# Routing the second part of a mixture-of-experts kernel in two batches in place of one

## What is computed

```python
x = x + conv(ln_c(x))              # per row i: q, k, v, gate g from 64 channels, 4 heads of 32
    # scores = q.k * scale + bias ; a = softmax(scores) ; o = g * (a.v) ; project back to 64 channels
t = x.reshape(64 * 128, 128)       # 8192 tokens
xf = layernorm(t)
gate_logits = xf @ Wg + bg                           # 8 experts
top_w, top_i = top_k(gate_logits, 2); top_w = softmax(top_w)
for e in range(8):
    h = gelu(xf @ W1[e] + b1[e])                     # 128 -> 512
    out += w_dense[:, e:e+1] * (h @ W2[e] + b2[e])   # 512 -> 128
return t + out
```

## Time and profile before

| | |
|---|---|
| median of three executions | 930.24 us (928.44 to 931.15) |
| the profiled execution | 927.51 us, of which 925.7 us from first to last instruction (the span) |
| busy, of the span | DVE 715.3 us (77%), PE 671.7 (73%), ACT 600.8 (65%), POOL 476.7 (52%) |
| granted TensorE clock, mean | 0.887 of full speed |
| chain that ended last | PE 54%, DVE 26%, issue 6%, POOL 6%, DMA 4%, SP's queue 2% |

### The profile page before, as it was taken

The page is one execution under the profiler, slowest core; times in us unless marked ns, Lnnn a source line. Parts: engine busy times, 40 slices in busy tenths (PEclk is TensorE's granted clock), DMA queues, the critical chain, the costliest instruction groups (busy, mean ns, idle before and its releaser), DMA issues.

```text
span 925.7 us, 22535 instructions
## 1 busy us (share of the span) xinstructions
PE 671.7 (73%) x7125; PEld 539.0 (58%) x7125; DVE 715.3 (77%) x2447; ACT 600.8 (65%) x1502; POOL 476.7 (52%) x550
## 2 busy tenths in 40 slices
PE   0006698988799678867897753629999999999900
PEld 0001477777577456646675642518888888888800
DVE  3798488888888797878777858478888888888843
ACT  0015489999699576856785674227888888888700
POOL 4000133444564356736865587005777777777770
PEclk9999699999899898978987875559999999999965
DMA  9932750000000000000000013225422214464178
GB/s 200 221 86 54 189 85 2 2 2 2 1 2 2 1 1 25 25 0 17 28 19 24 16 44 89 50 50 142 111 77 80 65 52 134 111 161 120 50 212 238
DMA packets 66936, 64.53 MB, mean 70 GB/s; under 512 B 21637, under 2 KB 58054, under 8 KB 65288
## 3 DMA queue, kind: packets, MB, share of 16 engines
q1 hardware_dynamic: 56392, 35.95, 16.7%
q0 software_dynamic: 9152, 18.76, 6.2%
q10 hardware_dynamic: 1280, 8.39, 4.0%
HBM read 35.88 MB, written 26.93 MB: 68 GB/s over the span
## 4 chain that ended last, share of the span: by engine, by line
PE 54%; DVE 26%; issue 6%; POOL 6%; DMA 4%; SPq 2%; ACT 1%; POOLq 0%; ACTq 0%; DVEq 0%
PE PT L1459 12%; PE S L1305 4%; PE PT L1315 4%; PE B L1343 4%; PE S L1444 4%; PE S L1446 4%; PE S L1445 4%; DVE L L969 3%; PE PT L1451 2%; DMA xt<-in_x 2%; DVE on L982 2%; PE A L1274 2%; DVE xt L990 2%; DVE pl L956 2%; POOL expert_out L698 2%
## 5 line engine op out<-in xcount | busy, mean ns | idle before, releaser
L857 ACT ACTIVATE hf<-S,b_sb,inv_hscale 128x256 f32<-128x256 f32 x312 | 150.8, 564 | 28.7 <-PE S L1446 28.7
L667 POOL DMA_INDIRECT routed<-pay,pos x128 | 127.5, 996 | 68.9 <-issue 31.5
L969 DVE CUSTOM_DVE_ANT_0 L<-S,biasN,logit_scale 128x128 f32<-128x128 f32 x512 | 148.3, 345 | 16.5 <-issue 14.9
L776 ACT ACTIVATE L<-L,lmin 128x128 f32<-128x128 f32 x512 | 159.2, 391 | 0.4
L651 POOL TENSOR_TENSOR og<-gt,on 128x256 f32<-128x256 f32 x64 | 46.5, 726 | 163.3 <-DVE on L982 163.1
L698 POOL DMA_INDIRECT expert_out<-pay x108 | 112.7, 1043 | 32.9 <-issue 26.5
L1212 DVE SCALAR_TENSOR_TENSOR hl<-hf,hscale,hh 128x512 f16<-128x512 f32 x156 | 117.2, 751 | 5.6
L1210 DVE TENSOR_SCALAR hh<-hf,hscale 128x512 f16<-128x512 f32 x156 | 75.4, 484 | 41.7 <-ACT hf L857 41.7
L771 ACT ACTIVATE ph<-PT 128x512 f16<-128x512 f32 x128 | 75.9, 595 | 27.8 <-PE B L1332 19.6
L1459 PE MATMUL PT<-w_h,hh 128*128 x624 | 86.5, 220 | 2.3 <-DVE hl L1212 2.3
L956 DVE TENSOR_TENSOR pl<-PT,ph 128x512 f16<-128x512 f32 x128 | 83.5, 682 | 4.6 <-ACT ph L771 4.6
(11 more groups left out here) (241 smaller groups left out, 1812.0 us busy)
## 6 DMA issues: line engine op xcount, KB each, us to landing
pay<-routed SPq DMA_DIRECT2D x54, 130.0 KB
shared<-expert_out SPq DMA_DIRECT2D x12, 384.0 KB, 6.6
xt<-in_x SPq DMA_DIRECT2D x8, 512.0 KB, 24.5
shared<-in_L_conv_ln_w ACTq DMA_DIRECT2D x8, 512.0 KB, 12.1
shared<-in_L_conv_ln_b ACTq DMA_DIRECT2D x8, 512.0 KB, 10.4
shared<-in_L_ffn_W SPq DMA_DIRECT2D x8, 512.0 KB, 7.2
routed<-blank SPq DMA_DIRECT2D x30, 129.0 KB, 2.6
shared<-expert_out SPq DMA_DIRECT2D x16, 224.0 KB, 5.5
```

The lines of the kernel that those rows point to most:

```text
L667: pool.indirect_dma_start(routed[TABLE_OF[b]], bass.IndirectOffsetOnAxis(ap=pos[k][:, row:row + 1], axis=0), source[:, part_row(b, i), :], ...
L776: last = nc.scalar.activation(L[p][:, h, i, :], L[p][:, h, i, :], ACT.Exp, scale=-1.0, bias=lmin[p][:, h * R + i:h * R + i + 1])
L857: last = nc.scalar.activation(hf[p][:, b, :], S[2 * p + pair][:, k * TILE:(k + 1) * TILE], ACT.Gelu, scale=inv_hscale[:, 0:1], bias=b1_fla ...
L969: last = nc.vector.tensor_tensor_reduce(out=L[p][:, h, i, :], in0=S[h][:, i * P:(i + 1) * P], in1=biasN[:, h, :], scale=logit_scale[:, 0:1 ...
```

## The change

The 24 rows of the fourth batch become a batch of 8 (rows 40 to 47) and a last one of 16 (rows 48 to 63). Both go to table 1, and the numbers of tiles, 47 and 31, are as they were.

- The batch of 8 is routed inside attention. By `plan` its `scale_rows` stands at the end of step 27, its rows at steps 28 and 29, turning at 29 and 30, gate logits at 30 and 31, the halves of `pick` at 31 and 32, ranks and positions at 33, ahead of `tile_table(0)` in the same step. The ranks of batch 2 stand in step 30 too; gate logits therefore get other columns of the bank (`GATE_AT`), and PE waits for DVE to have taken them before it starts the ranks.
- Its rows have a payload of their own for each choice, in `rows_all`: POOL normalises each row twice, and both choices can be sent without `second_choice`. Of its 16 transfers four stand in step 34, and the other twelve behind attention, after the twelve left of batch 2.
- The transition handles 16 rows in place of 24: four groups in place of six. The transfers among the tiles are 32 in place of 48, spread over the same 29 tiles.
- The slots of the tiles change order: `pay[0]` is used first and `rows_all` from the twentieth tile on, ahead of which SP waits for the 16 transfers. Buffers move (`L0`, the junk of the squares).

```diff
-    BATCHES = ((0, 16), (16, 12), (28, 12), (40, 24))
-    TABLE_OF = (0, 0, 0, 1)
+    BATCHES = ((0, 16), (16, 12), (28, 12), (40, 8), (48, 16))
+    TABLE_OF = (0, 0, 0, 1, 1)
+    LAST_BATCH = len(BATCHES) - 1
+    LATE_GROUP = BATCHES[LAST_BATCH][0] // 4
...
+    GATE_AT = 0
...
-        pay += [sbm(f"pay{k}", [P, PART_ROWS[1], ROW]) for k in (1, 2)]
+        pay += [sbm(f"pay{k}", [P, BATCHES[LAST_BATCH][1], ROW]) for k in (1, 2)]
...
-        slot = [rows_all[:, b] for b in range(EXTRA_SLOTS)] + [pay[0][:, 2 * b:2 * b + 2, :] for b in range(PART_ROWS[0] // 2)]
+        slot = [pay[0][:, 2 * b:2 * b + 2, :] for b in range(PART_ROWS[0] // 2)] + [rows_all[:, b] for b in range(EXTRA_SLOTS)]
...
-            for b, (first, n) in enumerate(BATCHES[:3]):
+            for b, (first, n) in enumerate(BATCHES[:LAST_BATCH]):
...
-            waiting = [[b, k, 0, rank_step[b] + 1 if k == 0 else None] for b in range(3) for k in range(2)]
+            waiting = [[b, k, 0, rank_step[b] + 1 if k == 0 or b == 3 else None] for b in range(LAST_BATCH) for k in range(2)]
...
+        def pay_of(b, k):
+
+            if b < 3:
+                return pay[0][:, BATCHES[b][0]:BATCHES[b][0] + BATCHES[b][1], :]
+            if b == 3:
+                return rows_all[:].rearrange("p b k w -> p (b k) w")[:, k * BATCHES[3][1]:(k + 1) * BATCHES[3][1], :]
+            return pay[1 + k][:]
...
             for t in range(8, PART_TILES[0]):
+                if t == PART_ROWS[0] // 2:
+                    for k in range(2):
+                        sp.wait_ge(scattered[3][k], 16 * BATCHES[3][1])
                 load_rows(t)
...
-                for i in range(g * R, (g + 1) * R):
-                    last = nc.gpsimd.tensor_scalar(pay[0][:, i, 0:W], xt[:, i, :], mean[:, i:i + 1], rstd[:, i:i + 1],
-                                                   ALU.subtract, ALU.mult)
+                b = batch_of(g)
+                for k in range(2 if b == 3 else 1):
+                    for i in range(g * R, (g + 1) * R):
+                        last = nc.gpsimd.tensor_scalar(pay_of(b, k)[:, i - BATCHES[b][0], 0:W], xt[:, i, :],
+                                                       mean[:, i:i + 1], rstd[:, i:i + 1], ALU.subtract, ALU.mult)
...
-            late = [(3, k, i) for k in range(2) for i in range(BATCHES[3][1])]
+            late = [(LAST_BATCH, k, i) for k in range(2) for i in range(BATCHES[LAST_BATCH][1])]
...
-            for g in range(10, GROUPS):
+            for g in range(LATE_GROUP, GROUPS):
                 normal_rows(g, pay[1])
...
                 if s in ranks_at:
+                    if s in gates_at:
+                        pe.wait_ge(lg_ready, gates_at[s] + 1)
                     rank(ranks_at[s], A)
```

More of the change, by code:

```diff
@@ L427, in scatter_plan @@
                         item[2] += 1
-                    if k == 0 and item[2] == BATCHES[b][1] and waiting[2 * b + 1][3] is None:
+                    if b < 3 and k == 0 and item[2] == BATCHES[b][1] and waiting[2 * b + 1][3] is None:
                         second_at.setdefault(min(s + 2, LAST - 1), []).append(b)
@@ L437, in meta_count, with batch_of @@
         def meta_count(b, k):
-            order = sorted([(rank_step[c], 0, c) for c in range(3)] + [(s, 1, c) for s in second_at for c in second_at[s]])
-            return order.index(next(o for o in order if o[1] == k and o[2] == b)) + 1
-        def part_row(b, i):
-            return BATCHES[b][0] + i - (PART_ROWS[0] if TABLE_OF[b] else 0)
+            if b == LAST_BATCH:
+                return 2 * 3 + 2
+            order = sorted([(rank_step[c], 0, c) for c in range(LAST_BATCH)] + [(s, 1, c) for s in second_at for c in second_at[s]])
+            return order.index(next(o for o in order if o[1] == (k if b < 3 else 0) and o[2] == b)) + 1
+        def pay_of(b, k):
[4 more added lines that the diff above has]
+            return pay[1 + k][:]
+        def batch_of(g):
+            return next(b for b, (first, n) in enumerate(BATCHES) if first <= g * R < first + n)
         def row_statistics(first, stop):
@@ L674, in step @@
                 if p == 1 and s < UNITS:
-                    for b in range(3):
+                    for b in range(LAST_BATCH):
                         for k in range(2):
@@ L1047, in take_logits @@
                 if g == 0:
-                    chain.link(nc.vector.tensor_copy(bgate_all[:], bank[:, RANK_AT + R * E:RANK_AT + (R + 1) * E]))
-                b = next(b for b, (first, n) in enumerate(BATCHES) if first <= g * R < first + n)
-                at = g * R - BATCHES[b][0]
-                nc.vector.tensor_tensor(lg[:, at:at + R, :], bank[:, RANK_AT:RANK_AT + R * E].rearrange("p (i e) -> p i e", e=E),
+                    chain.link(nc.vector.tensor_copy(bgate_all[:], bank[:, GATE_AT + R * E:GATE_AT + (R + 1) * E]))
+                at = g * R - BATCHES[batch_of(g)][0]
+                nc.vector.tensor_tensor(lg[:, at:at + R, :], bank[:, GATE_AT:GATE_AT + R * E].rearrange("p (i e) -> p i e", e=E),
                                         over(bgate_all[:], R), ALU.add).then_inc(lg_ready, 1)
@@ L1107, in positions @@
                     for j in range(2):
-                        chain.link(nc.vector.tensor_copy(pay[1 + j][:, :, W], weight[j][:, rows]))
-                        last = nc.vector.tensor_scalar(pay[1 + j][:].bitcast(I32)[:, :, W + 1], token_id[:, rows],
+                        chain.link(nc.vector.tensor_copy(pay_of(b, j)[:, :, W], weight[j][:, rows]))
+                        last = nc.vector.tensor_scalar(pay_of(b, j).bitcast(I32)[:, :, W + 1], token_id[:, rows],
                                                        float(j * TOKENS), None, ALU.add)
@@ L1172, in _ @@
             statistics(GROUPS - 1)
-            scale_rows(3)
-            for g in range(10, GROUPS):
+            scale_rows(LAST_BATCH)
+            for g in range(LATE_GROUP, GROUPS):
                 normal_rows(g, pay[1])
@@ L1188, in split_weights @@
                                                w_h[n][:].rearrange("p b e d -> p (b e d)"), ALU.mult, ALU.subtract).then_inc(w_split, 1)
-            for g in range(10, GROUPS):
+            for g in range(LATE_GROUP, GROUPS):
                 take_logits(g, B)
-            pick(3)
+            pick(LAST_BATCH)
             split_weights(0)
-            take_ranks(3, B)
-            positions(3)
-            tile_table(1, carry[4])
+            take_ranks(LAST_BATCH, B)
+            positions(LAST_BATCH)
+            tile_table(1, carry[LAST_BATCH + 1])
             split_weights(1)
@@ L1413, in _ @@
             pe.wait_ge(pl_ready, 4 * UNITS)
-            for g in range(10, GROUPS):
+            for g in range(LATE_GROUP, GROUPS):
                 wait(pe, xnT_ready, g - 1)
-                turn_rows(g, PT[g % 2], pay[1])
-                if g > 10:
+                turn_rows(g, PT[g % 2])
+                if g > LATE_GROUP:
                     wait(pe, lg_ready, g - 1)
```

34 lines of the change are left out of this document (17 added, 17 removed).

## The result

| | before | changed |
|---|---|---|
| time, first series: median (range) | 930.1 us (928.4 to 931.2) | 936.67 us (935.6 to 937.8) |
| time, second series, with the variants below | 929.94 us (927.6 to 931.6) | 938.12 us (936.5 to 938.5) |
| profiled execution: its time, span | 927.51 us, 925.7 us | 937.82 us, 936.1 us |

The change makes the kernel slower: 1.0073 times the time before, 95% interval 1.0052 to 1.0093, and 1.0082 (1.0066 to 1.0098) when it was measured again. That is 6.6 and 8.2 us. The forecast was 931.6, no change that can be told. That forecast failed: the time lies 5 us above it, and the intervals exclude no change. It is inside the range of 924 to 938; the second median, 938.12, lies just outside.

The account below looks back on a forecast made before the run. It took attention as a PE-DVE chain, the transition as DVE-led, tiles as PE-bound, and POOL as delaying the end by 5.5 us. Terms 15.1 - 8.2 - 5.5 = +1.4 us gave 931.6 us on the median, range 924 to 938.

Parts of the forecast that it names:

- The tail: After the tiles: 16 fewer POOL transfers let SP's loads follow its stores directly; gain 5.5 us, bounds 3 and 8.
- The transition: Between attention and tiles: fewer normalisations, two groups less and narrower pick pieces save 8.2 us, bounds 7 and 9.5.
- Scaling: Step 27: 18 small chained DVE instructions cost 6.9 us, modelled on step 11; at least 3.02 us.
- Rows at steps 28 and 29: Attention: 16 rows take POOL 13.1 us, nearly all covered; cost 0.8 us, between 0 and 13.1.
- POOL becomes the bound: Rival, steps 28 and 29: POOL's waits are no cover if DVE's outputs wait for POOL; 937.8 us, chance 0.22.
- the cover that was counted: Steps 28 to 30: scaling's delay 3.9, POOL's waits for DVE 6.2 and PE's wait 2.89, together 13.0 us.
- Its deciding point: Start of step 30: if `vl` still ends PE's wait there, POOL has not become the bound.
- Steps 30 to 33: Attention: logits ahead of ranks in step 30 1.2 us, step 31 2.5, step 32 nothing, step 33 3.7.
- The faster one: Rival: tail gains 2.5 us more from the third group's wait, scaling costs 3.0, not 6.9; 925.2 us, chance 0.20.
- The change does not free POOL: Rival: transfers moved behind attention push POOL's first sends back, costing the tail's 5.5 us; 937.1 us, chance 0.02.
- POOL's rows holding DVE's port: Rival: four two-operand pieces of `pick` each held up by a 0.82 us row operation; 3.3 us, 934.9 us, chance 0.06.
- the forecast's own case: Whole kernel: POOL's cover and work in steps 28 and 29 about even; 931.6 us, range 928 to 935, chance 0.50.

Follow-up runs that it names:

- the run with two scalings: The changed kernel with batch 3's scaling done twice, one behind the other, at the end of step 27: 940.88 us, ratio 1.0115 to the kernel before.
- ACT's copy: The changed kernel with POOL normalising batch 3's rows once and ACT making the second payload by one copy behind attention: 933.41 us, ratio 1.0040 to the kernel before.
- the later copy: The changed kernel with POOL's second copy of batch 3's rows made in steps 30 and 31: 934.37 us, ratio 1.0050 to the kernel before.
- the variant with the whole pick: Changed kernel with second payload copied by ACT, batch 3's turns and gates one step later, pick whole in step 32, ranks still in 33: 929.27 us, 0.9996.
- the variant with scaling in pieces: As the variant with the whole pick, plus batch 3's scaling in four pieces in step 28 and rows in steps 29 and 30: 923.26 us, ratio 0.9939.

## Why the prediction was right and wrong

**The tail: right mechanism, 1.6 to 1.9 us short.** The loads issue behind the stores, POOL's last send comes before them, and DVE's wait for the third group stays (5.40 us). The term was 5.5 and measured 3.6 to 3.9, near the lower bound, for the reason given for that bound: the loads share the engines with the stores. POOL's last send comes 7.6 us behind PE's last pass (893.91), not within the 5 us stated, but SP still issues stores then, until 911.19. The prediction speaks of 28 transfers left behind attention, 16 of them new; by the plan it is 24, 12 of them new. POOL still waits 19.73 us before its first send, so that slip cost nothing.

**The transition: right.** 8.2 forecast, 8.8 and 9.4 measured. Four logits 2.5 us apart are left of six, and the eight normalisations are gone.

**Scaling: right place, 1.1 us short.** 6.9 forecast, 8.0 measured. Step 11 was the right model; there too the three pieces beside POOL took 0.56, 0.60 and 1.16 us. The changed kernel's rows and the run with two scalings show what the number is made of: 5.6 us of the chain beside POOL and 2.4 for standing.

**Rows at steps 28 and 29: the term that failed.** "I take 0.8, between 0 and 13.1": it measured 4.3 (ACT's copy and the later copy agree). That is for the second eight. Without them POOL waits for DVE again, 0.85 us at the second `og` of step 30, and with turns, gates and pick moved as well stretches 29 and 30 are 16.08 and 15.91 us (16.78 and 15.91 before), so the first eight cost nothing that shows. The rival "POOL becomes the bound" named the flaw of the cover that was counted, that POOL's waits are cover only if DVE's outputs do not themselves wait for POOL. They did, through `gt`: `og` late, ACT's `gt` and `vh` late, `vl` late.

Its deciding point was badly drawn, though. It asks whether `vl` still ends PE's wait at the start of step 30 (2.89 us). It does not; the first projection of step 30 follows without a wait, since the turning of batch 3's rows now stands ahead of it and takes that wait, for `pl`:

```profile
514.68 1.12 PE L1367 MATMUL PT<-identity,rows_all 128*128 128x128 f32 x4 [2.38 <-DVE pl L974]
...
517.74 0.80 PE L1291 MATMUL A<-xs,w4h 128*128 128x512 f32 x1
```

With ACT's copy, where POOL is in time, it is the same (3.06 us for `pl` there), so this point could not decide. The wait that POOL's lateness added is PE's 2.88 us, one step earlier in PE's list, and its row names `vl` as well. A row names the last link; here POOL shows two links back, at ACT's 2.85 us.

**Steps 30 to 33: 7.4 forecast, 8.5 measured** (what is left: 20.8 - 8.0 - 4.3). The sum was near; what was missed is that 4.9 of it came from the places of batch 3's turns, gates and pick and could be avoided. I priced the logits ahead of the ranks in step 30 at 1.2 us; the waits in the rows are 0.57 and 0.91. The low clock of stretch 31 (0.65, and 0.80 before) is not theirs: with ACT's copy the wait of 0.57 us is still there, and the stretch has 0.83. Which of the moved pieces cost the rest stays open. The second half of the pick in step 32 was forecast at 0; the variant with the whole pick there bears it out.

**The rivals.** The faster one is out: the third group's wait stayed and scaling cost 8.0, not 3.0. "The change does not free POOL" is out by SP's rows. POOL's rows holding DVE's port is out too, and better shown than before. (The prediction's piece of 1.12 us at 483.87 in the earlier trace rows ran beside POOL's split `xs`, 483.60 to 484.87, and not beside `og`; both have two operands.) In the variant with scaling in pieces, DVE's and POOL's timelines:

```profile
485.33 1.00 DVE L1121 TENSOR_TENSOR r_a<-lg,top 128x96 f32<-128x96 f32 x1
486.37 0.26 DVE L1122 TENSOR_TENSOR r_b<-r_a,order 128x96 f32<-128x96 f32 x1
...
486.95 0.26 DVE L1125 TENSOR_TENSOR oh<-r_b,key 128x96 f32<-128x96 f32 x1
487.24 0.26 DVE L1127 SCALAR_TENSOR_TENSOR lg<-oh,lg 128x96 f32<-128x96 f32 x1
...
484.95 1.27 POOL L659 TENSOR_TENSOR xs<-xf,xs 64x512 fp32r<-64x512 f32 x1 [0.17 <-POOL og L671]
486.32 3.31 POOL L679 TENSOR_SCALAR rows_all<-xt,mean,rstd 128x128 f32<-128x128 f32 x4
```

Beside POOL's two-operand `xs` a piece of DVE took 1.00 us; the next three, beside POOL's rows, took 0.26. The Trainium skill, "SBUF — State Buffer", section "Who interferes with whom", has a DVE instruction with two SBUF inputs contend with any GpSimd instruction that reads SBUF; here a row operation with one tensor operand held none of these three up, and a two-operand one did. Elsewhere rows did cost a piece a little: one of 0.29 us took 0.42 at 314.86 in the kernel before.

**The sum.** Forecast +15.1 - 8.2 - 5.5 = +1.4. Measured +20.8 - 9.4 - 3.6 and small change, +8. Of the 6 to 7 us between them 3.5 are the rows, some 2 the tail, 1.1 each scaling and steps 30 to 33, less 1 for the transition. The range of 924 to 938 held because the POOL rival had been priced into it (6.2, measured 4.3); the forecast's own case, in which cover and work are even, was the one that failed.

## What to carry to other kernels

When work is added to an engine that "only waits", look at who waits for the outputs that come behind it in its queue, and follow each wait of the trace back until it reaches work and not another wait: idle time is cover only outside that ring. Moving a piece by one or two steps can be worth as much as making it cheaper: the second copy of the rows cost 4.3 us in two steps and nothing two steps later, while ranks moved past the last addition took nearly all of the gain back. Read the length of a chain of small instructions where it stands, and not from its shortest piece: 18 pieces that start 0.20 us apart elsewhere took 5.6 us beside POOL, and cost 8.0 where PE and ACT stood; the next 18 cost 3.5.

## What the runs showed of the hardware

- Executions of one program differ in the clock that they are granted at the same place: 133 passes of PE in step 15 took 11.64 us at 1.00 and 12.61 at 0.87, with the same work ahead of them. That moves steps 14 to 20 by up to 3 us, so one profile of each kernel is not enough for differences under 0.3%.
- A stall of 5.21 us on PE was followed by 6.35 us of passes at a clock of 0.56; in the whole stretch, at 0.76, the same 131 passes took 2.8 us longer than before, at 0.87.
- A piece of DVE with two operands took 1.16 us beside POOL's two-operand `xs` and 0.17 where POOL waited; beside POOL's rows, with one tensor operand, pieces of 0.26 us took 0.26.
- Transfers that start earlier on a busy set of DMA engines give back part of it: SP needed 11.53 us to issue the tail's 16 loads beside the end of the stores and 10.05 us when they started 5.5 us behind them.
